# A graph layer on one core: the first two rounds' edge offsets searched in the partition that needs them

## The chip, the core and the metric

The kernel runs on one core of a Trainium2 chip. The metric is the device time of one execution in microseconds (us). Three runs of the kernel before took 808.64, 809.55 and 809.91 us; their median is 809.55. Five engines work side by side, each on its own list of instructions: TensorE (PE), VectorE (DVE), ScalarE (ACT), GpSimd (POOL) and SyncE (SP, which only issues DMAs). Semaphores order them.

## The reference

There are 6250 nodes and 206250 edges, sorted by their target dst; every node has 128 features.

```python
h = x @ W_node.T + b_node
e = edge_attr @ W_edge.T + b_edge
msg = (h[src] + e) @ W_msg.T + b_msg
s = segment_sum(msg, dst)
deg = segment_sum(ones, dst)
out = layernorm(x + s / maximum(deg, 1)[:, None])
```

## The kernel before, in words

Both sums are made with matmuls against one-hot matrices. The nodes are treated in 25 groups of 250 (NB), called rounds; they begin with group 7 (G0), so round m is group (7 + m) mod 25, and N0 = 1750 is the first node of round 0.

**Edge features.** The edges are cut into 101 blocks of 2048 (SUP), from block 27 (FIRST) on. For block t, SP loads 1 MB of edge_attr into one of three buffers (`load_edges`, L375); DVE makes a one-hot of each edge's node relative to the first one of its quarter (`make_onehot`, L725); PE sums (`sum_windows`, L536); ACT copies the result (`copy_windows`, L1167ff); DVE makes `place`; PE puts the window at its nodes (`place_windows`, L549); DVE adds it to `sums_e` (`add_sums`, L736). The relative node numbers come from dst, which ACT loads as `dst_nat`, 2048 edges to a partition; DVE subtracts the first of each quarter and PE turns them.

**Node features.** For each round m, 125 partitions hold the edges of two nodes each. Their 125 entries of src are fetched by an indirect DMA at `clipped_int` (`load_window`, L472). `make_keys` (L764) turns them into a block and a row of x, PE turns these (`turn_keys`), ACT spreads them, DVE makes one-hots for 25 partitions at a time (`make_hots`, L746), a segment, five of which make a round; PE counts them (`count_fill`, L606), ACT moves the counts (`move_bank`), and PE multiplies the counts by x, which is split in three bf16 parts (`apply_counts`, L617). The split of x: ACT copies the high half (`copy_hi`, seven pieces), POOL subtracts it (`split_rest`, L484) and subtracts again (`split_low`, L490), seven times each. The first apply_counts waits for all of them.

**Where a node's edges begin.** This is what the change is about. There are three searches ("jobs"), for the 625 nodes of which rounds 0 and 1 need 500 (job 0), for the later nodes up to 6249 (job 1), and for nodes 0 to 1749 (job 2, called A). In each job 125 partitions have JOB_K nodes each (5, 31, 14). `block_counts` (DVE, L825) and `count_blocks` (PE, L516) count, per partition, the blocks of 128 edges that begin below its first node; `begin_job` (L830) makes an index of it, `load_job` (POOL, L465) fetches 375, 1375 or 750 entries of dst from there, `count_nodes` (DVE) and `sign_counts` (ACT) count in them for each node how many are below it, and `end_job` adds the parts. As a job's partitions hold other nodes than a round's partitions, the result is written to DRAM (`send_starts`, L1188), read back row by row (`fetch_starts`, L1194) and turned by PE (`turn_slots`, L566); `make_slots` (L871) then has slot and index for each round.

**The order.** It is written out by hand: a list of slots u, each engine runs through it in the same order. Slots 0 to 7 (LEAD) treat one edge block each; from slot 8 on, g = u - 8 is a segment, with a block in most of them. So round m has segments 5m to 5m + 4, and apply_counts of round 0 begins with segment 5. On SP, x is loaded behind block 3 (`load_x`, L388), the small weights behind block 6. In slot 6, before, DVE makes the keys of round 0, and behind slot 7 the one-hots of segment 0. POOL's list is: gathers of jobs 0, 1, 2, windows 0 and 1, seven split_rest, seven split_low, the later windows.

## Time and profile before

| what | us |
|---|---|
| median of three runs (808.64 to 809.91) | 809.55 |
| the profiled execution | 809.33 |
| its span, first to last instruction | 807.5 |
| PE busy | 732.5 |
| DVE busy | 634.8 |
| ACT busy | 462.2 |
| POOL busy | 80.5 |

The span is what the profile covers; the 1.8 us between 809.33 and 807.5 lie around it. Times in rows count from the span's start. PE is the engine that works most; where it isn't busy, something else sets the pace, and the slices show where that is.

### The profile page before, as it was taken

The page shows a single profiled execution, that of the slowest core. Times are in us where ns is not written, and L with a number is a line of the kernel's source. Part 1 is how long each engine was busy: PE and PEld are TensorE (multiplying, and loading weights), DVE is VectorE, ACT ScalarE, POOL GpSimd, SP SyncE. Part 2 cuts the span into 40 slices and gives each one's busy share as a digit, 9 for nine tenths or more (in the row PEclk, how much of TensorE's full clock was granted, in tenths as well). Part 3 has the DMA queues.
Part 4 walks back from the last instruction along what each step waited for, and adds up shares of the span by engine and source line. Part 5 has one row for each costly group of instructions (what it writes and reads, how often), then busy time and mean ns, then how long its engine had stood idle before and what let it go on. Part 6 is the DMA issues. An engine that isn't in the chain of part 4 may idle for free.

```text
span 807.5 us, 24927 instructions
## 1 busy us (share of the span) xinstructions
PE 732.5 (91%) x10573; PEld 647.3 (80%) x10573; DVE 634.8 (79%) x1137; ACT 462.2 (57%) x948; POOL 80.5 (10%) x63
## 2 busy tenths in 40 slices
PE   2634569999999999999999999999999999999995
PEld 2423457888988898888988888898898889888895
DVE  7518997699878878887898788878887887888732
ACT  4104955575666566655666576566565656665641
POOL 2113722001000000000000000000000000000000
PEclk9995759899999999999999999999999999999998
DMA  6984426263446424644354454445534653364200
GB/s 206 215 278 156 141 68 179 84 196 122 137 146 223 144 97 162 207 143 162 115 190 151 163 175 125 158 147 197 171 105 134 218 158 130 113 220 134 98 14 16
DMA packets 71806, 121.11 MB, mean 150 GB/s; under 512 B 4717, under 2 KB 17738, under 8 KB 71591
## 3 DMA queue, kind: packets, MB, share of 16 engines
q1 hardware_dynamic: 68462, 115.72, 44.4%
q0 software_dynamic: 2496, 2.84, 1.5%
q8 instruction: 87, 1.43, 0.7%
q10 hardware_dynamic: 734, 0.90, 0.5%
q14 instruction: 27, 0.22, 0.1%
HBM read 116.19 MB, written 3.23 MB: 148 GB/s over the span
## 4 chain that ended last, share of the span: by engine, by line
PE 84%; DVE 8%; DMA 3%; issue 2%; SPq 2%; DVEq 0%; ACT 0%; ACTq 0%
PE x_ps L628 48%; PE count_ps L613 18%; PE win_ps L545 12%; PE win_ps L552 3%; DMA edges<-in_edge_attr_dram 2%; SPq L392 2%; DVE key_hot L754 1%; PE misc_ps L639 1%; PE misc_ps L640 1%; DVE row_hot L754 1%; DVE onehot L728 1%; DVE dve_junk L849 1%; DMA region<-in_dst_dram 1%; DVE region L827 1%; DVE place L734 1%
## 5 line engine op out<-in xcount | busy, mean ns | idle before, releaser
L628 PE MATMUL x_ps<-region,x_rest 128*128 128x250 bf16 x2450 | 450.3, 270 | 0.0
L1227 ACT CAST region<-count_ps 128x490 bf16<-128x490 f32 x625 | 350.8, 574 | 164.4 <-PE count_ps L613 158.8
L628 PE MATMUL x_ps<-region,x_hi 128*128 128x250 bf16 x1225 | 333.0, 272 | 0.0
L754 DVE TENSOR_TENSOR row_hot<-iota_bf,row 125x3200 bf16<-125x3200 bf16 x125 | 229.6, 1837 | 86.5 <-PE count_ps L613 59.7
L613 PE MATMUL count_ps<-key_hot,row_hot 125*128 125x98 bf16 x3125 | 244.7, 210 | 13.4 <-DVE key_hot L754 13.3
L628 PEld LDWEIGHTS x_ps<-region,x_rest 128*128 128x128 bf16 x2450 | 230.0, 98 | 17.7
L613 PEld LDWEIGHTS count_ps<-key_hot,row_hot 125*128 125x128 bf16 x3125 | 200.1, 99 | 43.0 <-issue 18.5
L754 DVE TENSOR_TENSOR key_hot<-iota_bf,key 125x2500 bf16<-125x2500 bf16 x125 | 183.2, 1466 | 0.0
L545 PE MATMUL win_ps<-edges,onehot 128*32 128x128 f32 x3232 | 119.2, 293 | 18.4 <-DMA edges<-in_edge_attr_dram 16.6
L628 PEld LDWEIGHTS x_ps<-region,x_hi 128*128 128x128 bf16 x1225 | 119.1, 97 | 8.0
L545 PEld LDWEIGHTS win_ps<-edges,onehot 128*32 128x32 f32 x3232 | 89.2, 116 | 40.6 <-issue 38.9
L477 POOL DMA_INDIRECT win_src<-in_src_dram,clipped_int x25 | 44.6, 1782 | 539.5 <-DVE key_bf L783 417.7
L1171 ACT COPY win_sb<-win_ps 128x128 f32<-128x128 f32 x101 | 26.9, 266 | 109.2 <-PE win_ps L545 106.4
L728 DVE TENSOR_TENSOR onehot<-iota_bf,rel_col 128x512 f32<-128x512 bf16 x101 | 72.1, 714 | 0.0
L552 PE MATMUL win_ps<-place,win_sb 128*128 128x128 f32 x202 | 43.7, 301 | 15.9 <-ACT win_sb L1171 11.0
L552 PEld LDWEIGHTS win_ps<-place,win_sb 128*128 128x128 f32 x202 | 32.8, 204 | 19.5 <-ACT win_sb L1171 12.6
L744 DVE TENSOR_TENSOR sums_e<-sums_e,win_ps 128x128 f32 x101 | 28.8, 285 | 13.9 <-PE win_ps L552 6.7
L734 DVE TENSOR_SCALAR place<-iota_f,pos 128x128 f32<-128x128 f32 x101 | 33.3, 329 | 0.0
L1239 ACT ACTIVATE stddev<-mean_var,eps_col 125x2 f32<-125x2 f32 x25 | 7.4, 296 | 35.9 <-DVE mean_var L815 35.9
L1245 ACT ACTIVATE y<-y,shift,rstd 125x128 f32<-125x128 f32 x50 | 22.0, 490 | 0.9 <-DVE shift L822 0.9
L793 DVE SCALAR_TENSOR_TENSOR y<-misc_ps,recip,resid 125x128 f32<-125x128 f32 x50 | 15.1, 344 | 8.9 <-PE misc_ps L640 8.9
L639 PE MATMUL misc_ps<-w_both,sums_e 128*125 128x128 f32 x100 | 19.2, 274 | 0.5 <-issue 0.5
(166 smaller groups left out, 345.0 us busy)
## 6 DMA issues: line engine op xcount, KB each, us to landing
edges<-in_edge_attr_dram SPq DMA_DIRECT2D x101, 1024.0 KB, 5.7
resid<-in_x_dram SPq DMA_DIRECT2D x25, 125.0 KB
out_dram<-y SPq DMA_DIRECT2D x25, 125.0 KB
region<-in_dst_dram ACTq DMA_DIRECT2D x1, 768.0 KB
win_src<-in_src_dram,clipped_int POOLq DMA_INDIRECT x25, 6.7
region<-in_L_gnn_W_node_dram SPq DMA_DIRECT2D x1, 64.0 KB
region<-in_L_gnn_W_edge_dram SPq DMA_DIRECT2D x1, 64.0 KB
region<-in_L_gnn_W_msg_dram SPq DMA_DIRECT2D x1, 64.0 KB
```

The costliest lines, as they stand in the source:

```text
L477: pool.indirect_dma_start(out=win_src[:, m % 3, :], out_offset=None, in_=src.rearrange("(r e) -> r e", e=WE), in_offset=bass.IndirectOffse ...
L545: mm = pe.matmul(bank[q * W:(q + 1) * W, 0:D], hot[:, q * J + j, :], edges[:, t % EDGE_SLOTS, q * J + j, :], start=(j == 0), stop=(j == J ...
L552: pe.matmul(l2_ps[t % 2], win_sb[:, t % 2, :], place[:, t % 2, :], start=True, stop=True).then_inc(l2_done, 1)
L613: mm = pe.matmul(count_ps[fill % COUNT_BANKS][:, k * KEYS:(k + 1) * KEYS], row_hot[0:WE, g % 2, f * FILL + k, :], key_hot[0:WE, g % 2, f * ...
L628: mm = pe.matmul(x_ps[m % 2][:, 0:NB], rows, counts[m % 2][:, b, :], start=(n == 0), stop=(n == PARTS - 1))
L639: pe.matmul(to, sums_e[:, first + h * PB:first + (h + 1) * PB], w_both[:, 1, :], start=True, stop=False)
L728: dve.tensor_tensor(onehot[:, t % ONEHOT_SLOTS, :, :], iota_bf[:, 0:W].rearrange("p (a w) -> p a w", a=1).to_broadcast([P, TILES, W]), rel ...
L734: dve.tensor_scalar(place[:, t % 2, :], iota_f[:, :], pos[:, sup_of[t]:sup_of[t] + 1], None, ALU.is_equal).then_inc(place_ready, 1)
L744: dve.tensor_tensor(to, to, l2_ps[t % 2], ALU.add).then_inc(added, 1)
L754: ins = dve.tensor_tensor(hot[0:WE, g % 2, :, :].rearrange("p w (a b) -> p w a b", b=4), iota_bf[0:WE, 0:width].rearrange("p (c a b) -> p ...
L1171: act.copy(win_sb[:, t % 2, :], win_ps[t % 2][:, 0:D]).then_inc(win_copied, 1)
L1227: act.copy(counts[m % 2][:, :, f * FILL * 2:(f + 1) * FILL * 2], count_ps[fill % COUNT_BANKS][:, 0:FILL * KEYS].rearrange("p (n b) -> p b ...
```

## The change

A near search for rounds 0 and 1 takes the place of job 0. Partition p of round r searches itself for the starts of nodes N0 + 250 r + 2p, + 1 and + 2, the three that its slots need, in 275 entries of dst (`begin_near`, `load_near`, `find_near`), three compares on DVE; `take_slots` makes slot and index from them in the same partition. DRAM, ACT and PE's turning have no part in it. The starts are still written to DRAM, in segment 3 (`send_near`), for the degrees of all nodes. Two searches follow, with 32 and 14 nodes a partition and gathers of 1650 and 750 entries. The first local offsets go to PE quarter by quarter, with begin_near(0) between the second and the third. SP waits for all of dst before it loads block 0, and for the first near gather before it loads block 2. x is loaded in two pieces, 21 of its 49 blocks of 128 rows behind edge block 2, the others behind edge block 3. ACT's copies of x go from slots 5 to 7 and segments 0 and 1 to slot 7 and segments 0 to 2. The keys of round 0 move from slot 6 to 5, the one-hots of segment 0 from slot 7 to 6. Each near search has checks that join those already there.

```diff
-JOBS = 3
+JOBS = 2
+NEAR = 2
+NEAR_L = 275
...
-    JOB_K = (5, 31, 14)
-    JOB_N = (N0, N0 + PB * JOB_K[0], 0)
-    JOB_L = (375, 1375, 750)
-    JOB_DVE = (3, 13, 4)
-    JOB_ROWS = (2, B_ROUNDS - 2, G0)
-    JOB_ROUND = (0, 2, B_ROUNDS)
-    LOWEST = ((30, -60), (33, -220), (30, -60))
-    HIGHEST = ((36, 188), (33, 358), (36, 188))
-    TAIL = E - JOB_K[1] * 33 - 175
+
+    NEAR_HIGH = (36, 188)
+    JOB_K = (32, 14)
+    JOB_N = (N0 + NEAR * NB, 0)
+    JOB_L = (1650, 750)
+    JOB_DVE = (13, 4)
+    JOB_ROWS = (B_ROUNDS - NEAR, G0)
+    JOB_ROUND = (NEAR, B_ROUNDS)
...
-            def load_x():
-                sp.wait_ge(x_zeroed, 1)
-                whole = N // P
-                sp.dma_start(x_rest[:, 0:whole, :], x[0:whole * P, :].rearrange("(b p) d -> p b d", p=P)).then_inc(x_in_dram, 16)
-                sp.dma_start(x_rest[0:N - whole * P, whole, :], x[whole * P:N, :]).then_inc(x_in_dram, 16)
+            def load_x(i):
+                whole, half = N // P, 21
+                if i == 0:
+                    sp.dma_start(x_rest[:, 0:half, :], x[0:half * P, :].rearrange("(b p) d -> p b d", p=P)).then_inc(x_in[0], 16)
+                else:
+                    sp.wait_ge(x_zeroed, 1)
+                    sp.dma_start(x_rest[:, half:whole, :], x[half * P:whole * P, :].rearrange("(b p) d -> p b d", p=P)).then_inc(x_in[1], 16)
+                    sp.dma_start(x_rest[0:N - whole * P, whole, :], x[whole * P:N, :]).then_inc(x_in[1], 16)
...
+            sp.wait_ge(dst_in, 48)
             for t in range(NS):
+                if t == 2:
+                    sp.wait_ge(near_in[0], 16)
                 load_edges(t)
-                if t == 3:
-                    load_x()
+                if t in (2, 3):
+                    load_x(t - 2)
...
+            def load_near(r):
+                pool.wait_ge(near_ready[r], 1)
+                pass_waits()
+                pool.indirect_dma_start(out=win_near[r][0:PB, :], out_offset=None, in_=dst.rearrange("(r e) -> r e", e=NEAR_L),
+                                        in_offset=bass.IndirectOffsetOnAxis(ap=near_idx[r][0:PB, 0:1], axis=1)).then_inc(near_in[r], 16)
...
-                pool.wait_ge(src_index_ready, 1 + sum(1 for r in JOB_ROUND[1:] if m >= r))
+                pool.wait_ge(src_index_ready, m + 1 if m < NEAR else NEAR + sum(1 for r in JOB_ROUND if m >= r))
...
+                load_near(r)
+                load_window(r)
             for k in range(JOBS):
                 load_job(k)
-            for m in range(2):
-                load_window(m)
...
-            pe.wait_ge(rel_ready, 1)
             for q in range(Q):
+                pe.wait_ge(rel_ready, q + 1)
...
+            pe.wait_ge(count_taken, 1)
+            count_blocks(1)
...
-                        pe.wait_ge(count_taken, t + 1)
-                        count_blocks(t + 1)
-                    if t == 4:
-                        turn_slots(0)
+                        pe.wait_ge(count_taken, t + 2)
+                        count_blocks(t + 2)
                     place_windows(t)
-                    if t == 6:
+                    if t == 5:
...
+            def begin_near(r):
+                dve.wait_ge(counted, r + 1)
+                link(dve.tensor_scalar(near_base[r][:, 0:1], x_ps[0][0:PB, r:r + 1], float(BLOCK), -float(BLOCK), ALU.mult, ALU.add))
+                dve.sem_inc(count_taken, 1)
+                link(dve.tensor_scalar(near_base[r][:, 1:2], near_base[r][:, 0:1], 0.0, float(E - NEAR_L), ALU.max, ALU.min))
+                dve.tensor_copy(near_idx[r][:, :], near_base[r][:, 1:2]).then_inc(near_ready[r], 1)
...
+            def find_near(r):
+                dve.wait_ge(near_in[r], 16)
+                for i in range(3):
+                    hi = NEAR_HIGH[0] * i + NEAR_HIGH[1]
+                    nodes[0] += 1
+                    if nodes[0] > 2:
+                        dve.wait_ge(node_counted, nodes[0] - 2)
+                    dve.tensor_scalar(dve_junk[nodes[0] % 2][0:PB, 0:hi], win_near[r][0:PB, 0:hi], near_node[r][:, i:i + 1], None, ALU.is_lt, ALU.add,
+                                      accum_out=near_cnt[r][:, i:i + 1]).then_inc(node_counted, 1)
+                dve.wait_ge(node_counted, nodes[0])
+                link(dve.tensor_scalar(near_start[r][:, :], near_cnt[r][:, :], near_base[r][:, 1:2], None, ALU.add))
+                take_slots(r, 1, near_start[r][:, :].rearrange("p (i g) -> p i g", g=1))
...
+            def take_slots(r, rows, found):
+                at = slice(r, r + rows)
+                link(dve.tensor_copy(first_slot[:, :, at], found))
...
-            ins.then_inc(rel_ready, 1)
-            begin_job(0)
-            block_counts(1)
+                ins.then_inc(rel_ready, 1)
+                if q == 1:
+                    begin_near(0)
...
+            block_counts(1)
             dve.wait_ge(pos_turned, 1)
             dve.tensor_copy(base_int[:, :], misc_ps[0:1, 128:128 + NS])
             dve.tensor_copy(check_junk[0:1, 0:NS], misc_ps[0:1, 256:256 + NS])
             link(dve.tensor_copy(pos[:, :], misc_ps[:, 0:NS]))
+            make_place(0)
+            dve.wait_ge(rel_copied, 2)
+            make_onehot(0)
+            make_onehot(1)
+            find_near(0)
             link(dve.scalar_tensor_tensor(check_junk[0:1, 0:NS - 2], misc_ps[0:1, 385:384 + NS - 1], 0.0, check_junk[0:1, 0:NS - 2], ALU.add, ALU.is_lt,
                                           accum_out=viol[0:1, 3:4]))
-            dve.wait_ge(rel_copied, 2)
-            make_onehot(0)
-            make_place(0)
-            make_onehot(1)
+            begin_near(1)
             block_counts(2)
...
-                        begin_job(t + 1)
                     if t == 1:
-                        count_nodes(0, 0, JOB_DVE[0])
-                        end_job(0)
+                        begin_job(0)
+                        block_counts(3)
                     if t == 2:
+                        find_near(1)
+                        begin_job(1)
+                    if t == 3:
                         check_sorted()
-                    if t == 3:
-                        check_job(0)
                     if t == 4:
-                        make_slots(0)
-                    if t == 6:
+                        check_near(0)
+                        check_near(1)
+                    if t == 5:
                         make_keys(0)
...
-                if u == LEAD - 1:
+                if u == LEAD - 2:
                     make_hots(0)
...
+            def send_near():
+                act.wait_ge(src_index_ready, NEAR)
+                for r in range(NEAR):
+                    act.dma_start(starts_dram[N0 + r * NB:N0 + (r + 1) * NB].rearrange("(p k) -> p k", k=2), near_start[r][:, 0:2]).then_inc(near_sent, 16)
...
+                act.wait_ge(x_in[0], 16)
+                if i >= 3:
+                    act.wait_ge(x_in[1], 32)
...
-                        sign_counts(0, JOB_DVE[0], JOB_K[0])
-                    if t == 2:
-                        send_starts(0)
-                    if t == 3:
-                        fetch_starts(0)
-                    if t >= 5:
-                        copy_hi(t - 5)
-                    if t == 6:
+                    if t == 5:
                         spread_keys(0)
+                    if t == 7:
+                        copy_hi(0)
                     continue
...
-                if g < 2:
-                    for i in range(3 + 2 * g, 5 + 2 * g):
+                if g < 3:
+                    for i in range(1 + 2 * g, 3 + 2 * g):
                         copy_hi(i)
-                if g < 3:
-                    sign_counts(1, [13, 19, 25][g], [19, 25, 31][g])
+                    sign_counts(0, [13, 19, 25][g], [19, 25, 32][g])
                 if g == 3:
+                    send_starts(0)
+                    send_near()
```

How it moves instructions. The first place is DVE from where it takes the turned positions to the second block_counts; `misc_ps` is what PE turned, `lent` holds small constants, `region` the gathered entries. Before:

```order
L983 COPY pos<-misc_ps 128x101
L984 SCALAR_TENSOR_TENSOR check_junk,viol<-misc_ps,check_junk 1x99
L728 TENSOR_TENSOR onehot<-iota_bf,rel_col 128x512
L734 TENSOR_SCALAR place<-iota_f,pos 128x128
L728 TENSOR_TENSOR onehot<-iota_bf,rel_col 128x512
L827 TENSOR_TENSOR region<-block_first,lent 101x2000
L832 TENSOR_SCALAR job_base<-x_ps 125x1
```

and now:

```order
L1038 COPY pos<-misc_ps 128x101
L760 TENSOR_SCALAR place<-iota_f,pos 128x128
L754 TENSOR_TENSOR onehot<-iota_bf,rel_col 128x512 x2
L901 TENSOR_SCALAR dve_junk,near_cnt<-region,near_node 125x188
L901 TENSOR_SCALAR dve_junk,near_cnt<-region,near_node 125x224
L901 TENSOR_SCALAR dve_junk,near_cnt<-region,near_node 125x260
L904 TENSOR_SCALAR near_start<-near_cnt,near_base 125x3
L926 COPY first_slot<-near_start 125x3
L927 TENSOR_SCALAR clipped_int<-first_slot 125x1
```

The search of round 0 and its slots stand before the sums of the first window; before, its three compares came in slot 1 and its slots in slot 4.

The second place is DVE at the end of the lead, from a window's sum to the second pair of one-hots. Before, slot 7:

```order
L744 TENSOR_TENSOR sums_e<-sums_e,win_ps 128x128
L734 TENSOR_SCALAR place<-iota_f,pos 128x128
L728 TENSOR_TENSOR onehot<-iota_bf,rel_col 128x512
L754 TENSOR_TENSOR row_hot<-iota_bf,row 125x3200
L754 TENSOR_TENSOR key_hot<-iota_bf,key 125x2500
L754 TENSOR_TENSOR row_hot<-iota_bf,row 125x3200
```

and now, from slot 6 on:

```order
L754 TENSOR_TENSOR onehot<-iota_bf,rel_col 128x512
L780 TENSOR_TENSOR row_hot<-iota_bf,row 125x3200
L780 TENSOR_TENSOR key_hot<-iota_bf,key 125x2500
L763 TENSOR_LOAD base_int
L763 ISA x2
L770 ISA
L770 TENSOR_TENSOR sums_e<-sums_e,win_ps 128x128
L760 TENSOR_SCALAR place<-iota_f,pos 128x128
```

A window's sum stands between the one-hots of segment 0 and those of segment 1.

The third place is SP's first loads. Before:

```order
L373 DMA region<-in_dst_dram 1x1198
L378 DMA edges<-in_edge_attr_dram 128x4x512 x4
L391 DMA x_rest<-in_x_dram 128x48x128
L392 DMA x_rest<-in_x_dram 106x128
L378 DMA edges<-in_edge_attr_dram 128x4x512 x3
```

and now:

```order
L386 DMA region<-in_dst_dram 1x1231
L391 DMA edges<-in_edge_attr_dram 128x4x512 x3
L404 DMA x_rest<-in_x_dram 128x21x128
L391 DMA edges<-in_edge_attr_dram 128x4x512
L407 DMA x_rest<-in_x_dram 128x27x128
L408 DMA x_rest<-in_x_dram 106x128
```

One edge block stands between the pieces of x, and block 4 is still behind both.

## Rows read from the trace of the kernel before

**Rows 1.** The page: busy time, and two of its lines of 40 slices

```profile
PE 732.5 (91%) x10573; PEld 647.3 (80%) x10573; DVE 634.8 (79%) x1137; ACT 462.2 (57%) x948; POOL 80.5 (10%) x63
...
PE   2634569999999999999999999999999999999995
```

**Rows 2.** Stretch from 200 to 400 us: busy by engine, clock, DMA share, GB/s

```profile
200.00:400.00 200.00, 200.00 (x2988) 178.86 (x2987) 168.00 (x269) 125.47 (x256) 12.91 (x7) 1.00 0.48 155
```

**Rows 3.** Timeline of PE, 52 to 80 us: start, length, line, what, [idle before, releaser]

```profile
52.85 1.94 PE L545 MATMUL win_ps<-edges,onehot 128*32 128x128 f32 x32 [16.65 <-DMA edges<-in_edge_attr_dram]
...
56.16 1.94 PE L545 MATMUL win_ps<-edges,onehot 128*32 128x128 f32 x32
...
65.37 0.36 PE L602 MATMUL misc_ps<-ident_bf,row_bf 125*125 125x125 bf16 x1 [3.06 <-DVE key_bf L783]
...
74.68 2.31 PE L613 MATMUL count_ps<-key_hot,row_hot 125*128 125x98 bf16 x25 [5.79 <-DVE key_hot L754]
```

**Rows 4.** Timeline of SP's queue at 35 us

```profile
35.23 9.14 SPq L378 DMA_DIRECT2D edges<-in_edge_attr_dram  x1
```

**Rows 5.** Stretches of the lead: the last two columns are DMA share and GB/s

```profile
10.00:12.00 2.00, 1.54 (x15) 1.55 (x15) 1.96 (x6) 0.00 (x0) 0.00 (x0) 1.00 1.04 386
20.00:22.00 2.00, 2.00 (x28) 1.62 (x21) 1.74 (x1) 0.27 (x1) 0.00 (x0) 1.00 0.07 6
38.00:40.00 2.00, 0.00 (x0) 0.00 (x0) 0.00 (x0) 0.00 (x0) 0.00 (x0) 1.00 1.09 185
42.00:46.00 4.00, 0.00 (x0) 0.00 (x0) 0.00 (x0) 0.00 (x0) 0.00 (x0) 1.00 0.66 141
```

**Rows 6.** Timeline of DVE, 52 to 75 us: the first one-hots for counting

```profile
71.44 1.81 DVE L754 TENSOR_TENSOR row_hot<-iota_bf,row 125x3200 bf16<-125x3200 bf16 x1
...
74.54 1.81 DVE L754 TENSOR_TENSOR row_hot<-iota_bf,row 125x3200 bf16<-125x3200 bf16 x1
```

**Rows 7.** Timeline of DVE, 7 to 30 us: the first use of dst

```profile
7.74 0.18 DVE L960 CAST block_first<-region 101x16 f32<-101x16 int32 x1 [0.45 <-DMA region<-in_dst_dram]
```

**Rows 8.** Line 469, the first two gathers (ns), and all three's time to landing

```profile
L469 POOL DMA_INDIRECT region<-in_dst_dram,job_idx x2: 1294/1798/2302, 14.4 to 24.3; - x2
...
DMA to landing us min/median/max: 5.5/20.3/23.0
```

**Rows 9.** Timeline of DVE: a window's turn on DVE, and a later one-hot

```profile
57.26 0.29 DVE L744 TENSOR_TENSOR sums_e<-sums_e,win_ps 128x128 f32 x1 [0.83 <-DVE slot_low L882]
...
57.66 0.68 DVE L728 TENSOR_TENSOR onehot<-iota_bf,rel_col 128x512 f32<-128x512 bf16 x1
...
61.63 2.38 DVE L728 TENSOR_TENSOR onehot<-iota_bf,rel_col 128x512 f32<-128x512 bf16 x1
```

**Rows 10.** Line 378, loads issued from 50 to 60 us

```profile
DMA to landing us min/median/max: 7.0/7.2/7.3
```

**Rows 11.** Timeline of POOL: the split of x, first subtractions

```profile
59.71 3.73 POOL L484 TENSOR_TENSOR x_rest<-x_rest,x_hi 128x896 f32<-128x896 f32 x2
...
78.66 3.73 POOL L484 TENSOR_TENSOR x_rest<-x_rest,x_hi 128x896 f32<-128x896 f32 x2 [7.83 <-ACT x_hi L1210]
87.84 3.74 POOL L484 TENSOR_TENSOR x_rest<-x_rest,x_hi 128x896 f32<-128x896 f32 x2 [5.45 <-ACT x_hi L1210]
```

**Rows 12.** Timeline of DVE, 101 to 108 us: end of job 1, segment 4's one-hots

```profile
102.81 0.23 DVE L856 TENSOR_TENSOR job_rel<-job_cnt,job_off 125x13 f32<-125x13 f32 x1
...
107.33 1.82 DVE L754 TENSOR_TENSOR row_hot<-iota_bf,row 125x3200 bf16<-125x3200 bf16 x1 [0.24 <-DVE bias_row L928]
```

**Rows 13.** Timeline of ACT: a copy of x, and the last sign pass of segment 2

```profile
67.94 0.94 ACT L1210 COPY x_hi<-x_rest 128x896 bf16<-128x896 bf16 x1
...
99.80 0.77 ACT L1185 ACTIVATE act_junk<-region,job_half 125x578 bf16<-125x578 int32 x1
```

**Rows 14.** Timeline, 104 us on: the first product of counts and x

```profile
115.07 0.41 PE L628 MATMUL x_ps<-region,x_hi 128*128 128x250 bf16 x1
```

**Rows 15.** Line 490: the seven low subtractions (ns, min/median/max)

```profile
L490 POOL TENSOR_TENSOR x_rest<-x_rest x7: 1677/1679/3261, 91.5 to 104.6; 128x896 bf16<-128x896 f32 x7
```

133 lines of the change are left out of this document (73 added, 60 removed).

## Prediction

> **What bounds the kernel now.** I read the page first, then stretches of the trace. The busy line gives TensorE (PE) 732.5 of 807.5 us, and the 40 slices show where it is missing: slices 0 to 5, that is the first 120 us, hold the idle time, from slice 8 on each has a 9 [rows 1]. In the stretch from 200 to 400 us PE is busy 200.00 of 200.00 us [rows 2]. The change touches no matmul of that part, so only what happens before the first rounds run at full pace can change the time: the question is by how much the start of the steady part moves.
>
> The start has three pieces. (a) DMA: behind x on SP's queue stand the edges of block 4, issued at 35.23, and PE stands 16.65 us for them, until 52.85 [rows 3, 4]. I call this moment T. While x moves, the DMA engines are full (share 1.09) at only 185 GB/s, against 386 GB/s while edges move [rows 5]. (b) From T a chain: the offsets of rounds 0 and 1 come back from DRAM and are turned only behind window 4, then their windows of src are fetched, keys made, and PE turns them at 65.37 after 3.06 us of waiting; DVE makes one-hots from 71.44 and PE's first counting starts at 74.68 [rows 3, 6]. (c) From 74.54 on DVE has one-hots, searches and sums in a row. So two points count: T, and the start of the second one-hot pair on DVE, 74.54 [rows 6], which is T + 21.7.
>
> **The early part, before T.** SP now waits for all of dst before the edges of block 0. DVE was through with its preparation at 7.3 and held by dst 0.45 us more [rows 7]; the small operations of a third job (some 0.5 us, an estimate) go too, so the chain starts about 0.9 us earlier. The first gather was issued at 14.4 and landed 5.5 us later [rows 8]. Its index now comes before half of the local offsets, about 1.0 us earlier in all: issue 13.4, landing 18.9. SP holds block 2 for it: its data start near 20.4, where before block 3's started near 22.2 (share 0.07 in 20 to 22 [rows 5]). So the DMA engines set out 1.8 us earlier, but with one more block before them: 1.05 MB at 386 GB/s is 2.7 us. The gathers that fall after this point are larger: before, 124 x 1375 and 125 x 750 words, 1.06 MB; now 124 x 1650, 125 x 750, 125 x 275 and two windows of 125 x 125, 1.46 MB. The 0.4 MB at some 300 GB/s are 1.3 us. x is cut in two, but all of it stays ahead of block 4, so the cut moves nothing for T. **T moves by -1.8 + 2.7 + 1.3 = +2.2 us, to 55.05.** Bounds: in 42 to 46 the share is only 0.66, engines that ran dry while others were behind [rows 5]. That is 1.4 us of full work; if the block laid between the pieces avoids it, and 0.8 us of the gathers slip in beside the x packets, T stays at 52.85. If the engine that is behind now carries more, T may reach 58.
>
> In the shadow of T: DVE now has two find_near (three compares and seven small operations each) and a fourth block_counts, and PE waits for the latter two. PE was idle for 16.65 us there [rows 3], and all of it fits in, if the second near gather comes. Its counterpart, issued at 24.3 among the x packets, took 23.0 us [rows 8]. So I expect it at about 47; behind it come find_near and begin_job (some 3 us, an estimate), add_sums, place and one-hot (1.1 [rows 9]) and PE's placing, to about 52. This is hidden by about 3 us and not more. The Trainium skill (DMA: Bandwidth & Descriptors, Queues, rings and completion order) says that an engine takes turns between its queue rows packet by packet; by that a 0.14 MB gather would come back in about the 5.5 us of the first one, and T would stay 55. No number of the sum needs it.
>
> **From T on.** A block costs PE and ACT 56.16 - 52.85 = 3.3 us [rows 3]. Keys and slots are long there, so nothing waits: blocks 4, 5 and 6 and the turned keys (0.4) end at T + 10.3. add_sums, place and one-hot take 1.1 us on DVE (57.26 to 58.34 [rows 9]) and are through at T + 11.6. The one-hots of segment 0 now stand in slot 6: 3.1 us [rows 6], to T + 14.7. Block 7 lies beside it; its load goes out when window 4 is summed, T + 1.9, and such loads land in at most 7.3 us [rows 10], T + 9.2; PE wants them at T + 10.3, so they are covered, by 1 us. Then 1.1 us for block 7 on DVE, T + 15.8. The first x split on GpSimd falls there; before, three of them fell into the chain [rows 11]: a one-hot took 2.38 us in place of 0.68 [rows 9]. I count half of one collision, 0.7. The second one-hot pair starts at **T + 16.5 and not T + 21.7: 5.2 us gained**. PE's first counting starts at T + 14.9 and not T + 21.8.
>
> **After that**, DVE's list is the same: 17 compares of both jobs, the same one-hots, so the 32.8 us to the one-hots of segment 4 (107.33 - 74.54 [rows 6, 12]) stay. ACT gets two more copies of x in segment 2, 0.94 us each, and one more sign pass of 0.77: 2.7 us [rows 13]. Its passes ended at 99.80 + 0.77 and DVE used them at 102.81 [rows 12, 13], 2.2 us of cover; ACT also starts its segment 0 by 4.7 us earlier where DVE starts 3.0 earlier, so 2.2 + 1.7 - 2.7 = 1.2 us of cover remain. Without it the addition would cost up to 2.7 us. The DMAs of near starts (two issues on ACT) and the waits of later windows lie before round 2 and are needed by nobody earlier; I set them at nothing. **Sum: -5.2 + 2.2 = -3.0 us.** The profiled execution took 809.33 us at a span of 807.5; 806.3 and 804.5 come out. The three runs before have the median 809.55, 0.2 above the profiled one, so I say **806.5 us**.
>
> **Rivals.** *The load tail vanishes.* T stays at 52.85 and the whole 5.2 us come through; with the collision gone too, 5.9 us: 803.7 us. For it speaks the share of 0.66 with work waiting [rows 5], against it that block 4 still stands behind every x packet. *Nothing gained.* The transfers are a floor: block 2 held for near_in, larger gathers among blocks 4 to 7, the second near gather at 52 or later and not at 47. It needs T to move by 5.2, to 58.05; then 809.6. For it: the gathers that were issued beside x took 20.3 and 23.0 us [rows 8]; against it: the added bytes are only 4 us of work. *Slower: x is split too late.* GpSimd splits x in 14 operations, and PE's first product with x at 115.07 needs all [rows 14]. Before, the rests 5 and 6 were done at 91.58. Now their copies stand one segment later; a segment is 87.84 - 78.66 = 9.2 us [rows 11]; with 4.7 us of lead they end at 96.1. Seven low subtractions follow, 1.68 to 3.26 us each [rows 15]; they now lie beside the one-hots of segments 4 and 5. Ready is 107.9 to 118.9, wanted is 115.07 - 3.0 = 112.1. It decides from 2.3 us each; their median was 1.68. At 3.26 PE waits 6.8 us and the kernel is 3.8 us slower: 813.3. For it: a one-hot that met a subtraction grew by 1.7 us and some of GpSimd's nearly doubled [rows 9, 15], and one-hots are the longest that DVE has; against it: half of the low subtractions would have to pay in full. The Trainium skill (SBUF — State Buffer, SBUF: two separate sides) calls the port pair that DVE and GpSimd share an exclusive lock: with two inputs in SBUF beside a reading GpSimd operation, the second one waits for the whole instruction. The step from 0.68 to 2.38 us agrees; by that rule alone all seven would pay and 813.3 would be the time.
>
> **How the numbers follow.** A measurement can tell about 0.2% (1.6 us) from no change. My case (gains of 1.6 to 4.5 us) gets 0.50, the vanishing tail 0.12, nothing gained 0.20, slower 0.18. Faster 0.62, same 0.20, slower 0.18. The range goes from 802.0 (the vanishing tail at 803.7, and the 1.4 us of dry engines gained on top) to 812.0 (two thirds of the late split's wait); about a tenth is left out on each side.
>
> **What would show it.** Right: the sum of window 4 begins at 53 to 57; no wait before the turned keys; first counting 14 to 16 us after T; from there on the same picture as before, moved. PE keeps 200.00 of 200.00 in the middle. Wrong in the early part: window 4 begins after 58, or PE waits for place there (the second near gather). Wrong in the late part: the first product with x waits for GpSimd, or ACT's sign passes are what DVE waits for in segment 2. If T comes before 51 I have misread what the x load costs.

## The result and the profile after

The changed kernel takes 813.62 us (median of 5 runs, 812.78 to 815.12) against 809.55 (808.51 to 810.24, 5 runs) for the kernel before, measured beside it. The ratio is 1.0055, 95% interval 1.004 to 1.007: slower, where 806.5 and a range of 802 to 812 had been predicted. The profiled span grew by 4.3 us, from 807.5 to 811.8.

The page of the changed kernel, busy time and PE's slices (answers to [rows 1]): up to the last slice, which has a 5 before and after, all the idle time is again ahead of slice 8.

```profile
PE 735.5 (91%) x10586; PEld 649.8 (80%) x10586; DVE 640.4 (79%) x1149; ACT 462.1 (57%) x946; POOL 84.8 (10%) x65
...
PE   4525549899999999999999999999999999999995
```

The timeline of PE in the lead, same columns as [rows 3]:

```profile
42.40 1.94 PE L577 MATMUL win_ps<-edges,onehot 128*32 128x128 f32 x32 [3.15 <-DMA edges<-in_edge_attr_dram]
47.34 1.94 PE L577 MATMUL win_ps<-edges,onehot 128*32 128x128 f32 x32 [1.83 <-DMA edges<-in_edge_attr_dram]
...
63.64 1.93 PE L577 MATMUL win_ps<-edges,onehot 128*32 128x128 f32 x32 [12.98 <-DMA edges<-in_edge_attr_dram]
67.92 1.94 PE L577 MATMUL win_ps<-edges,onehot 128*32 128x128 f32 x32 [1.18 <-DMA edges<-in_edge_attr_dram]
71.14 2.31 PE L641 MATMUL count_ps<-key_hot,row_hot 125*128 125x98 bf16 x25
```

These are the sums of windows 4 to 7 (the window of a block of edges has the block's number) and the first counting. Window 4 is summed at 42.40, 10.5 us sooner than before (52.85) and 12.7 sooner than I said. But the long wait for edges did not go: it stands in front of window 6 now, 12.98 us, and the counting starts only 3.5 us earlier than before (74.68).

Stretches of the lead, the last two columns being DMA share and GB/s, as in [rows 5]:

```profile
40.00:44.00 4.00, 1.60 (x32) 1.51 (x32) 2.63 (x13) 0.00 (x0) 1.92 (x2) 1.00 1.00 334
44.00:48.00 4.00, 1.79 (x26) 1.20 (x21) 2.29 (x9) 0.27 (x1) 0.00 (x0) 1.00 1.12 195
48.00:52.00 4.00, 2.28 (x28) 1.64 (x20) 1.13 (x4) 1.32 (x3) 0.00 (x0) 1.00 1.13 171
52.00:56.00 4.00, 0.00 (x0) 0.00 (x0) 0.00 (x0) 0.00 (x0) 0.00 (x0) 1.00 1.06 164
56.00:60.00 4.00, 0.00 (x0) 0.00 (x0) 0.00 (x0) 0.00 (x0) 0.00 (x0) 1.00 0.85 181
```

and the DMA issues from 38 us on (last number: us from issue to landing):

```profile
region<-in_dst_dram,job_idx POOLq DMA_INDIRECT x1, 25.9
...
win_a<-in_dst_dram,job_idx POOLq DMA_INDIRECT x1, 24.6
```

From 24 to 44 us, in which most of x and blocks 3 to 5 move, each stretch of 4 us has 282 to 334 GB/s. The stretch at 160 to 200 GB/s with full engines is still there; it begins at 44, behind x, when the two big gathers, issued at 38.6 and 40.4, are at work. That does not look like x.

The timeline of DVE for the one-hots (L754 makes a block's, L780 those for counting, L760 is place), with [rows 6, 12] as the counterpart:

```profile
73.60 1.81 DVE L780 TENSOR_TENSOR row_hot<-iota_bf,row 125x3200 bf16<-125x3200 bf16 x1
75.33 3.13 DVE L780 TENSOR_TENSOR key_hot<-iota_bf,key 125x2500 bf16<-125x2500 bf16 x1
...
93.50 3.50 DVE L780 TENSOR_TENSOR row_hot<-iota_bf,row 125x3200 bf16<-125x3200 bf16 x1
96.92 3.13 DVE L780 TENSOR_TENSOR key_hot<-iota_bf,key 125x2500 bf16<-125x2500 bf16 x1
100.17 1.50 DVE L760 TENSOR_SCALAR place<-iota_f,pos 128x128 f32<-128x128 f32 x1
101.60 2.18 DVE L754 TENSOR_TENSOR onehot<-iota_bf,rel_col 128x512 f32<-128x512 bf16 x1
...
111.27 2.27 DVE L780 TENSOR_TENSOR row_hot<-iota_bf,row 125x3200 bf16<-125x3200 bf16 x1 [0.24 <-DVE bias_row L982]
```

and of POOL, the split of x:

```profile
71.10 1.89 POOL L513 TENSOR_TENSOR x_rest<-x_rest,x_hi 128x896 f32<-128x896 f32 x1 [28.88 <-ACT x_hi L1275]
75.12 5.09 POOL L513 TENSOR_TENSOR x_rest<-x_rest,x_hi 128x896 f32<-128x896 f32 x2 [2.13 <-ACT x_hi L1275]
84.30 3.92 POOL L513 TENSOR_TENSOR x_rest<-x_rest,x_hi 128x896 f32<-128x896 f32 x2 [4.08 <-ACT x_hi L1275]
93.44 5.30 POOL L513 TENSOR_TENSOR x_rest<-x_rest,x_hi 128x896 f32<-128x896 f32 x2 [5.22 <-ACT x_hi L1275]
98.70 13.17 POOL L519 TENSOR_TENSOR x_rest<-x_rest 128x896 bf16<-128x896 f32 x7
```

The second pair starts at 73.60, 0.9 us earlier than before (74.54). From there to segment 4's one-hots it is 111.27 - 73.60 = 37.7 us; it was 32.8. Wherever POOL is at x, a place takes 1.5 to 1.7 us and not 0.28, a block's one-hot 2.2 to 2.4 and not 0.68, a key_hot 3.13 and not 1.45. **The sum: -0.9 + 4.9 = +4.0 of the 4.3 us.** PE's first product with x comes at 119.47 (115.07 [rows 14]), 4.4 us later; it waits for DVE's one-hots, not for x. From there to the end of the span the two kernels take the same time, 692.3 and 692.4 us. In the stretch from 200 to 400 us PE is busy 199.75 of 200 us.

The time behind that first product is not quite the same in all the profiled runs that follow: it lies between 688.6 and 693.1 us, with no order that the edits explain. So where two versions differ by 2 to 4 us, the traces' times up to the first product with x say how much of it is the edit's.

### The profile page after: what moved, and what is told of

Read it like the earlier page. It is cut to its first block, busy times and chain, and to the rows that moved or that the text cites. A ratio compares the mean times of both kernels' runs of the same rounds, so it can differ in the third digit from the quotient of the medians.

```text
span 811.8 us, 24971 instructions
## 1 busy us (share of the span) xinstructions
PE 735.5 (91%) x10586; PEld 649.8 (80%) x10586; DVE 640.4 (79%) x1149; ACT 462.1 (57%) x946; POOL 84.8 (10%) x65
## 4 chain that ended last, share of the span: by engine, by line
PE 84%; DVE 9%; DMA 4%; issue 2%; DVEq 0%; ACT 0%; ACTq 0%
PE x_ps L656 48%; PE count_ps L641 17%; PE win_ps L577 12%; DMA edges<-in_edge_attr_dram 3%; PE win_ps L584 3%; DVE key_hot L780 2%; PE misc_ps L667 1%; PE misc_ps L668 1%; DVE onehot L754 1%; DVE row_hot L780 1%; DVE region L853 1%; DVE dve_junk L882 1%; DVE place L760 1%; PE x_ps L549 1%; DMA region<-in_dst_dram 1%
## 5 line engine op out<-in xcount | busy, mean ns | idle before, releaser
L780 DVE TENSOR_TENSOR row_hot<-iota_bf,row 125x3200 bf16<-125x3200 bf16 x125 | 230.0, 1840 | 86.5 <-PE count_ps L641 59.7
L656 PEld LDWEIGHTS x_ps<-region,x_rest 128*128 128x128 bf16 x2450 | 230.1, 98 | 17.7
L780 DVE TENSOR_TENSOR key_hot<-iota_bf,key 125x2500 bf16<-125x2500 bf16 x125 | 185.2, 1481 | 0.0
L754 DVE TENSOR_TENSOR onehot<-iota_bf,rel_col 128x512 f32<-128x512 bf16 x101 | 72.2, 715 | 0.0
L760 DVE TENSOR_SCALAR place<-iota_f,pos 128x128 f32<-128x128 f32 x101 | 32.5, 322 | 0.0
L549 PE MATMUL x_ps<-ones_bf,region 101*125 101x1 bf16 x64 | 7.4, 245 | 17.5 <-DVE region L853 17.5
L549 PEld LDWEIGHTS x_ps<-ones_bf,region 101*125 101x125 bf16 x64 | 7.1, 227 | 18.7 <-DVE region L853 9.8
```

What stands on the lines that cost most here:

```text
L549: mm = pe.matmul(x_ps[0][0:PB, k:k + 1], before_hot[k][0:NS, j, :], ones_bf[0:NS, 0:1], start=(j == 0), stop=(j == TILES - 1))
L656: mm = pe.matmul(x_ps[m % 2][:, 0:NB], rows, counts[m % 2][:, b, :], start=(n == 0), stop=(n == PARTS - 1))
L754: dve.tensor_tensor(onehot[:, t % ONEHOT_SLOTS, :, :], iota_bf[:, 0:W].rearrange("p (a w) -> p a w", a=1).to_broadcast([P, TILES, W]), rel ...
L760: dve.tensor_scalar(place[:, t % 2, :], iota_f[:, :], pos[:, sup_of[t]:sup_of[t] + 1], None, ALU.is_equal).then_inc(place_ready, 1)
L780: ins = dve.tensor_tensor(hot[0:WE, g % 2, :, :].rearrange("p w (a b) -> p w a b", b=4), iota_bf[0:WE, 0:width].rearrange("p (c a b) -> p ...
```

## Experiments on the split of x

Theory P: all of the loss behind the second pair is POOL's split, now beside DVE's densest stretch, because ACT's copies of x, which release it, were moved from slots 5 to 7 and segments 0 and 1 to slot 7 and segments 0 to 2.

**The copies put back** (in the changed kernel), `e1_copies_back`:

```diff
-                    if t == 7:
-                        copy_hi(0)
+                    if t >= 5:
+                        copy_hi(t - 5)
...
-                if g < 3:
-                    for i in range(1 + 2 * g, 3 + 2 * g):
+                if g < 2:
+                    for i in range(3 + 2 * g, 5 + 2 * g):
```

> The changed kernel, with ACT's seven copies of x where they were before: slots 5, 6, 7 and segments 0 and 1. Theory P (the split of x on GpSimd, moved from the lead into the segments, costs DVE about 5 us there): the stretch from the second one-hot pair on DVE to the one-hots of segment 4, 37.7 us in the changed kernel, goes back to 33 to 34 us and the time to about 809 (808 to 810). Rival (it is ACT's extra work in segment 2, or the near searches, and the place of the split is nothing): 813 to 814.

Measured: 809.73 us, ratio to before 1.0017 (1.0003 to 1.003), against 1.0055: 3 to 4 us less than the changed kernel. The stretch is 31.9 us (75.95 to 107.89). The part of the change that cost time is the place of seven copies. But the time only comes back to the kernel before. The pair starts at 75.95, 2.4 us later than in the changed kernel, because two of POOL's subtractions now fall ahead of it, where a place took 1.69 us and a key_hot 3.13. So with its copies in the old place the change gains nothing either.

**All copies in slots 4 and 5**, `v1_split_in_lead`:

```diff
+                    if t == 4:
+                        for i in range(3):
+                            copy_hi(i)
                     if t == 5:
                         spread_keys(0)
+                        for i in range(3, 7):
+                            copy_hi(i)
...
```

The copies at slot 7 and in segments 0 to 2 go.

> The changed kernel with all seven copies of x in slots 4 and 5, so that GpSimd splits x while PE and DVE stand for the edges of block 6. Theory P: GpSimd is through by about 70 us, the stretch from the second one-hot pair to the one-hots of segment 4 shrinks to 24 to 28 us, the time is 800 to 805. Rival (the segments are paced by ACT's sign passes and the split's place matters little): 809 to 813.

Measured: 803.22 us, ratio 0.9932 (0.9904 to 0.996), faster than both kernels. POOL splits from 45.19 to 77.56. Four of the seven first subtractions (54.99 to 62.39) fall where DVE waits 8.45 us for window 6. The low ones, 62.35 to 77.56 and not done by 70 as expected, meet DVE at the first pair (row_hot 3.30 us, key_hot 2.93), so the second pair starts no earlier than in e1, 2.3 us later than in the changed kernel. In the stretch only that pair's row_hot meets POOL, and it is 25.4 us (75.94 to 101.32).

**The converse, in the kernel before**: copies at slot 7 and segments 0 to 2, `e4_before_copies_late`.

> The kernel before, with only the copies of x moved as in the change: slot 7 and segments 0 to 2 in place of slots 5 to 7 and segments 0 and 1. Theory P: slower by 2 to 5 us, 811 to 815 (the lead gains about 2 us that the segments lose again and more). Rival (place is nothing): 809 to 810.

Measured: 810.69 us, ratio 1.0023 (1.0005 to 1.0041). That is 1.9 us by the ratio, a little under the 2 to 5 expected. The second pair starts at 72.57, 2.0 us sooner than in the kernel before. The stretch grows only from 32.8 to 33.8 us, because POOL's operations met few one-hots in it: one row_hot took 3.29 us and one 2.08, while every place and key_hot up to 92 us took its undisturbed time. The loss stands behind the stretch, where the low subtractions (98.72 to 113.02) reach segment 4's one-hots: row_hot 2.27 us, key_hot 2.93, place 1.50. The first product with x comes at 117.25, and it was 115.07. So the same edit costs about 2 us there and 3 to 4 here. By the rows this hangs on which of DVE's operations POOL then meets.

## Experiments on the slow stretch

**A quarter of the big gathers**, `e2_gather_quarter`: 32 of the 125 partitions are fetched, the others hold a constant. The offsets of rounds 2 and later follow from the constant, and the fallback, the slow path for offsets that are not as assumed, is kept off.

```diff
-                n = PB - 1 if k == 0 else PB
+                n = 32
```

> The changed kernel; the two big gathers fetch 32 partitions instead of 124 and 125, the others hold a constant, and the flag for the slow path is always 0, so the offsets of later rounds are wrong. Theory G (the gathers, 1.2 MB in 249 long rows, make the slow stretch of DMA from 44 to 62 us, and x is not slow): that stretch shrinks to about a quarter, window 6 starts at 50 to 54 and not at 63.6, the time falls by 6 to 10 us to 804 to 808. Rival X (x's short rows or the tiny bias loads make it slow): the stretch stays at 160 to 180 GB/s and window 6 starts at 60 to 63; the time falls by 1 to 3 us.

Measured: 800.52 us, ratio 0.9896 (0.9874 to 0.9918). Window 6 comes at 53.19 with no wait. The stretch from 44 to 60 us:

```profile
44.00:60.00 16.00, 11.07 (x138) 8.22 (x138) 8.46 (x28) 2.95 (x7) 0.80 (x2) 1.00 1.06 333
```

The mechanism held; the gain on the changed kernel (0.9896 against 1.0055, 12.9 us) is larger than the 6 to 10 us expected. Window 6 comes 10.5 us earlier, as expected, the second pair as much (62.98), and segment 4's one-hots 12.1 us earlier (99.21).

**The same bytes by plain transfers, the same rows by indirect ones.** `e5_direct` takes fixed rows, one behind the other, without an index; `e8_indirect_apart` takes the same rows with an index that holds their places; `e9_indirect_overlap` lets the rows overlap (row p starts at word 1056 p and 448 p). All three fetch other words of dst than the search wants; the fallback is off. The edit of e5:

```diff
-                pool.indirect_dma_start(out=win_of[k][0:n, :], out_offset=None, in_=dst.rearrange("(r e) -> r e", e=JOB_L[k]),
-                                        in_offset=bass.IndirectOffsetOnAxis(ap=job_idx[k][0:n, 0:1], axis=1)).then_inc(job_win_in[k], 16)
+                pool.dma_start(win_of[k][0:n, :],
+                               dst[0:n * JOB_L[k]].rearrange("(r e) -> r e", e=JOB_L[k])).then_inc(job_win_in[k], 16)
```

> The changed kernel, but its two big gathers fetch the same number of bytes by plain transfers on GpSimd's queue: each partition gets a row of 1650 (750) words at a fixed place of dst, the rows do not overlap, and no index is read; the waits and the place in the program are the same. The words are not the ones wanted, so the offsets from round 2 on are not right, and the fallback is kept off. Theory I (what is slow is the indirect form, or windows of dst that overlap): 44 to 60 us runs at over 260 GB/s, window 6 is summed at 52 to 55 and not at 63.6, and the time is 801 to 806. Theory B (1.2 MB on a second queue in long rows into 124 partitions are slow in any form): 44 to 60 stays at 160 to 200 GB/s, window 6 at 61 to 65, time 812 to 815.

> The changed kernel, its two big gathers still indirect, but with fixed indices: row p starts at word 1650 p (750 p), so the rows lie one behind the other, as in the plain transfers of the run before. The offsets from round 2 on are not right and the fallback is kept off. The plain form took the slow stretch away; two things had changed with it, the indirect form and the overlap of the rows. Theory F (the indirect form is slow): 44 to 60 us stays at 160 to 210 GB/s, the gathers land 20 us or more after their issue, window 6 at 60 to 65, time 808 to 814. Theory O (overlapping windows are slow): over 260 GB/s, window 6 at 50 to 55, time 799 to 804.

> As the run before, but row p starts at word 1056 p (448 p): the rows overlap as the wanted ones do (by 594 of 1650 and 302 of 750 words), and all start at multiples of 256 or 64 bytes. Theory F: as the run before, 160 to 210 GB/s in 44 to 60, time 808 to 814. Theory O: slow here and fast in the run before. If both are fast, what is slow is the start of a row at any word and not at an even boundary.

| version | time, us | ratio to before (95%) | window 6 at | the gathers land after |
|---|---|---|---|---|
| e5_direct | 801.94 | 0.9907 (0.9872 to 0.9942) | 54.74 | 10.9, 12.4 us |
| e8_indirect_apart | 811.46 | 1.0028 (1.001 to 1.0046) | 63.83 | 25.7, 24.3 us |
| e9_indirect_overlap | 811.05 | 1.0031 (1.0014 to 1.0049) | 56.59 | 26.1, 24.9 us |

It is the indirect form: e5 and e8 fetch the same rows. In e9 window 6 came at 56.59, but window 7 then waited 7.96 us more and came at 67.66, as in e8 (67.54) and in the changed kernel (67.92): the lateness goes to one block or the next. The plain form is not free either: in e5 window 5 came at 51.49, after a wait of 5.66 us, and in the changed kernel at 47.34. The DMA queues from 38 to 66 us (packets, MB, share of 16 engines), first of e5_direct (plain):

```profile
DMA packets 4667, 8.74 MB, mean 312 GB/s; under 512 B 538, under 2 KB 928, under 8 KB 4664
...
q1 hardware_dynamic: 4376, 7.44, 79.3%
q0 software_dynamic: 288, 1.26, 18.2%
```

and of e8_indirect_apart:

```profile
DMA packets 3962, 6.32 MB, mean 226 GB/s; under 512 B 1008, under 2 KB 1393, under 8 KB 3961
...
q1 hardware_dynamic: 3161, 5.04, 72.6%
q0 software_dynamic: 800, 1.26, 23.1%
```

q1 is the queue that SP's loads use, q0 the gathers'. 1.26 MB of the same rows are 288 packets in the plain form and 800 in the indirect one, and the packets under 512 bytes go from 538 to 1008. The edges on q1 suffer too: 28 us of 16 engines, times 0.726, over 3161 packets is 103 ns for each, against 81 ns in the plain run, at about the same 1.6 to 1.7 KB. These slower packets are the larger part of the loss: at 81 ns each, q1's time in e8 would have held some 4000 packets, so some 850 of the 1215 by which q1 falls short are theirs, while q0's own share grew only from 18.2% to 23.1%. Why a packet of q1 is slower beside the indirect ones no row shows.

**Was it the same in the kernel before?** `e10_before_plain` is that kernel with the edit of e5 for jobs 1 and 2 (other words of dst, fallback off).

> The kernel before, its gathers of jobs 1 and 2 fetched by plain transfers of the same bytes (fixed rows, no index); their offsets are not right and the fallback is kept off. My prediction read 28 to 48 us of the kernel before as x being slow (185 GB/s). If it was the indirect gathers there too, x and the edges behind it move at over 260 GB/s, window 4 is summed at 42 to 47 and not at 52.85, and the time is 798 to 804. If x was slow by itself, window 4 stays at 50 or later and the time at 806 or more.

Measured: 802.65 us, ratio 0.9939 (0.9923 to 0.9956). The wait for block 4 on PE, where [rows 3] had 52.85 after 16.65:

```profile
46.77 1.94 PE L548 MATMUL win_ps<-edges,onehot 128*32 128x128 f32 x32 [10.77 <-DMA edges<-in_edge_attr_dram]
```

and the stretch in which x moves, first of the kernel before, then of e10:

```profile
28.00:44.00 16.00, 4.82 (x64) 3.29 (x56) 7.25 (x22) 0.53 (x2) 1.22 (x1) 1.00 1.02 193
```

```profile
28.00:44.00 16.00, 4.97 (x68) 3.43 (x60) 7.04 (x24) 0.53 (x2) 0.57 (x1) 1.00 1.05 265
```

So 6.1 us of T in the kernel before were the gathers. The drop from 265 to 193 GB/s, which I had read as the price of x, was two gathers that happened to move with it. The rest of the wait, 10.77 us, stays: x and block 4 behind it still have to move.

**Two smaller parts.** `e6_small_later` issues the weights and biases behind block 7 (`if t == 7: load_small()`), `e7_x_whole` both pieces of x behind block 3 (`if t == 3: load_x(0); load_x(1)`).

> The changed kernel, but the weights and biases (three transfers of 64 KB in rows of 512 bytes, and some of 4 bytes a row) are issued behind the edges of block 7 and not of block 6. Theory S (a good part of the slow stretch from 44 to 60 us is these small packets): the rate there rises over 240 GB/s, window 7 is summed by 62, the time is 806 to 810. Theory G (the big gathers make it): window 6 stays at 62 to 65, the time at 812 to 815.

> The changed kernel, but both pieces of x are issued behind the edges of block 3, one after the other, as x was before. Theory G (the gathers of dst set the start, the cut of x moves nothing): window 3 is summed some 2 us earlier, windows 4 to 7 where they were within 1.5 us (42.4, 47.3, 63.6, 67.9), the time 812 to 815. Rival (a block between the pieces costs or saves): windows 6 and 7 move by 2 us or more, and the time with them.

Measured for e6: 810.64 us, ratio 1.0023 (1.0003 to 1.0044), between the times of both theories, with the slow stretch still at 159 to 196 GB/s and window 6 at 61.34 (63.64). The small loads don't make the stretch. They cost little: of the some 3 us only 1.3 stand ahead of the first product with x (118.19), the rest behind it, where the edit changed nothing. For e7: 812.25 us, ratio 1.0048 (1.0032 to 1.0065), a time that can't be told from the changed kernel's. Window 3 came no earlier (36.05) and window 6 at 65.32, 1.7 us later, a little more than the 1.5 allowed.

## Versions made from this

**Gathers behind block 6** (v1, and POOL waits for block 6's landing before it issues them), `v2_gathers_behind`, and the same kernel once more, `v2_again`:

```diff
+            pool.wait_ge(edge_in[0], 16 * 3)
             for k in range(JOBS):
                 load_job(k)
```

> The version with all of x's copies in slots 4 and 5, and the two big gathers are issued only when the edges of block 6 have landed. Theory G: block 6 lands some 6 us after its issue, window 6 is summed at 50 to 54 and not at 59.3; the gathers then meet block 7 alone. If the loss does not just move on, the second one-hot pair starts by 68, nothing waits for the gathers, and the time is 796 to 801. Rival (it only moves on: block 7 or the first searches wait as long): window 7 is summed at 66 or later, or DVE waits for the gather in segment 0, and the time stays at 802 to 805.

> The version with the gathers behind block 6, once more. If the stall of DVE belongs to this order of GpSimd's work, one place operation stands again for 20 us or more, until the last of GpSimd's 14 split operations; if it was a chance of that execution, none stands over 4 us and the time is under 803.

Measured: 805.59 us, ratio 0.9961 (0.994 to 0.9982), slower than v1 and outside both expectations, and 807.65 in the one run of v2_again. Window 6 came at 48.54, even before the 50 to 54 expected, and window 7 at 54.00; then something that I had not foreseen. DVE and POOL of v2_gathers_behind:

```profile
54.41 21.81 DVE L761 TENSOR_SCALAR place<-iota_f,pos 128x128 f32<-128x128 f32 x1
76.14 0.68 DVE L755 TENSOR_TENSOR onehot<-iota_bf,rel_col 128x512 f32<-128x512 bf16 x1
```

```profile
50.52 1.22 POOL L492 DMA_INDIRECT win_a<-in_dst_dram,job_idx  x1 [0.30 <-issue]
51.76 12.91 POOL L513 TENSOR_TENSOR x_rest<-x_rest,x_hi 128x896 f32<-128x896 f32 x7
64.64 11.50 POOL L519 TENSOR_TENSOR x_rest<-x_rest 128x896 bf16<-128x896 f32 x7
```

A place operation of 0.28 us stood for 21.8 us, until the last of POOL's 14 operations ended at 76.14. v2_again shows the same, 21.58 us: it belongs to this order of work.

**A gate against it**, `v6_gate`: POOL waits, behind its gathers, for the one-hot that DVE makes behind window 7's sum (`pool.wait_ge(onehot_ready, 10)`).

> The version with the gathers behind block 6 (805.6), in which a place operation stood 21.8 us until GpSimd's 14th split operation was through; now GpSimd waits behind its gathers until place and one-hot of window 7 are done. If the stall came from the split starting right behind the issue of the gathers, no operation of DVE takes over 4 us, the second pair starts at 62 to 68, time 794 to 799. If DVE can be kept out by any unbroken run of GpSimd's operations, another one of its operations stands for 10 us or more and the time is 802 to 808.

Measured: 803.86 us, ratio 0.9942 (0.9924 to 0.9959). No operation of DVE stood over 3.1 us, and the second pair started at 59.50. But the gathers still took 23 us, and DVE then waited for the first one:

```profile
72.72 0.58 DVE L884 TENSOR_SCALAR_CACHE_REDUCE dve_junk<-region,job_node 125x358 bf16<-125x358 int32 x1 [10.03 <-DMA region<-in_dst_dram,job_idx]
```

and after it the low subtractions met its one-hots. The stall was gone, the gain was given back: the expectation failed by its time (794 to 799) and held by its operations. It doesn't fully clear the cause either: from 59.67, when POOL's split began, to 83.39 DVE had no place to do.

**The split as early as x allows**, `v3_split_early` and `v3_again`: ACT copies in slots 1 and 3, and POOL's list is

```diff
+            load_near(0)
+            load_window(0)
+            load_near(1)
+            split_rest(0)
+            split_rest(1)
+            load_window(1)
+            load_job(0)
+            load_job(1)
+            pool.wait_ge(onehot_ready, 7)
+            split_rest(2)
+            pool.wait_ge(keys_ready, 1)
+            for i in range(3, 7):
+                split_rest(i)
+            for i in range(7):
+                if i == 5:
+                    pool.wait_ge(onehot_ready, 9)
+                split_low(i)
```

> All of x's copies in slots 1 and 3 on ScalarE; GpSimd splits x piece by piece as early as it is there (two pieces ahead of the second src window, one behind window 4, the rest behind the keys of round 0), the big gathers where the changed kernel has them. Window 6 still waits for its edges until 58 to 62 (it is the gathers that hold it), but DVE's one-hots from there on are at 1.8 and 1.45 us and not at 3.3 and 2.9: the second pair starts at 67 to 72 (75.9 with the copies in slots 4 and 5), segment 4's one-hots at 92 to 97, time 796 to 800. Rival (DVE was not what followed behind: block 7 lands late, PE waits for it): second pair at 75, time 802 to 804.

> The best version once more, with more rounds: 793 to 798, ratio to before 0.981 to 0.988; window 7 at 66 to 69, second one-hot pair at 71 to 73.

Measured: 795.5 us, ratio 0.9846 (0.9807 to 0.9886), and in a second set of runs 798.44, ratio 0.9881 (0.9854 to 0.9908), window 7 at 69.15 and the second pair at 73.39, each a little beyond what was expected of it. The first product with x comes at 103.74 and 105.05, 15.7 and 14.4 us before the changed kernel's; by the ratios the two sets gain 16.9 and 14.1. POOL in v3_split_early:

```profile
29.15 4.68 POOL L513 TENSOR_TENSOR x_rest<-x_rest,x_hi 128x896 f32<-128x896 f32 x2 [4.68 <-ACT x_hi L1283]
...
48.95 7.84 POOL L513 TENSOR_TENSOR x_rest<-x_rest,x_hi 128x896 f32<-128x896 f32 x4 [1.01 <-DVE key_bf L817]
56.74 14.75 POOL L519 TENSOR_TENSOR x_rest<-x_rest 128x896 bf16<-128x896 f32 x7
```

The split is through at 71.5, the second pair starts at 72.10, segment 4's one-hots at 96.00: 23.9 us for what took 37.7. The first pair still met POOL, against the expectation (row_hot 3.29 us, key_hot 2.93), but it stands in the wait for window 7, where it costs nothing. Window 7 still comes at 66.89, after 10.46 us of waiting for edges, which is the gathers' part and stays. This version beats both kernels.

**Three tries on top.** `v4_early_and_behind` has the gathers behind block 6 too, with the last five low subtractions held until DVE has made the one-hot behind window 7's sum; `v5_second_last` issues the second gather behind the split; `v7_small_later` loads the weights behind block 7.

> As the run before, and the big gathers are issued behind block 6's landing (49 us), with the rest of the splits behind the keys and the last five subtractions behind the one-hot of window 9, so that DVE gets its turn between them. Window 6 at 48 to 50, window 7 at 54 to 56, no operation of DVE over 5 us, second pair at 62 to 68; then DVE waits for the first big gather until about 70. Time 793 to 800. If a place operation again stands until GpSimd's last subtraction (21.8 us in the version with the gathers behind), the time is 804 to 808 and the waits that were put in don't help.

> The version that splits x early (795.5), with the second gather (job 1) issued behind the whole split, at some 70 us; it is wanted at 103. One gather is left beside blocks 6 and 7: its packets end some 6 us earlier, window 7 is summed at 58 to 63 and not at 66.9, the second one-hot pair starts at 66 to 70 (72.1), time 790 to 794. Rival (DVE beside GpSimd's split sets the pair, not the edges): second pair at 71 to 72, time 795 to 796.

> The best version with the weights and biases issued behind block 7. In the changed kernel this edit freed window 6 by 2.3 us (61.3 for 63.6) and window 7 by 1.0. If block 7 is held by packets of the small loads ahead of it, window 7 is summed 1 to 3 us earlier than in the run before, time 793 to 795 where it has 795.5; if the gathers alone hold it, no difference over 0.2% to the run before.

Measured: 797.58 (ratio 0.9855, 0.9824 to 0.9887), 797.77 (0.9872, 0.9849 to 0.9896) and 799.36 us (0.9879, 0.9851 to 0.9906). None is told apart from v3. In v7 window 7 came 2.8 us earlier than in v3_again (66.35 for 69.15), the second pair did not (73.99 for 73.39), since DVE's key_hot and place there met POOL's last operations. In v4 a place stood again, for 9.35 us from 51.80, until POOL paused at 61.06, and window 7 came at 62.00 and not at 54 to 56. v5 is a miss of its own: with only one gather in the way window 7 came at 68.78, no earlier, and that gather took 27.1 us, while the second, issued at 72.04, landed in 7.2; from 72 to 80 us one block of edges was issued and all queues together moved 271 GB/s. The same gather (750 words a partition) had taken 24.6 us in the changed kernel. So the time of a gather follows what moves beside it more than its bytes, and one is enough to spoil the lead.

## Why the prediction was wrong

- **The early part up to the first gather: right.** Issue at 13.40 (13.4 predicted), landing after 4.3 us at 17.7 (18.9), block 2 issued at 17.8.
- **"While x moves ... only 185 GB/s": this step failed, and with it T.** The rate was put down to x; e10 has 265 GB/s where the kernel before had 193, with x moving all the same, and e5 and e8 show that it is the indirect form of the gathers of dst that slows the others. They are issued at 38.6 in the changed kernel and not at 24.3, so x and blocks 4 and 5 got ahead of them. T is 42.40, and not 55.05; it lies below my whole range for it, and "if T comes before 51 I have misread what the x load costs" was the right alarm.
- **The second near gather at about 47: wrong**, it landed 10.1 us after its issue, at 32.4. The 23 us came from a big gather, and this one was small. The 10.1 are also not the 5.5 that I had worked out by the Trainium skill (DMA: Bandwidth & Descriptors, Queues, rings and completion order).
- **Blocks 4, 5 and 6 at 3.3 us each and block 7 covered by 1 us: wrong**, for the same reason. Block 6 landed 25.5 us after its issue, where [rows 10] gave 7.3. The slow stretch had not been removed, it had moved behind T.
- **The second pair at T + 16.5 = 71.55: 2.0 us off** (73.60), from two errors that nearly cancel, by luck: T 12.7 us too late, what follows it 14.7 too short. The step gave 0.9 of the 3.0 us.
- **That the 32.8 us stay: this term cost the sign.** It was 37.7. I had counted half of one collision between POOL and DVE ahead of the pair and none after it, although [rows 9] showed the size, 1.7 us for one, and the diff showed the copies moved by one to two segments. I followed the copies only to the question whether x is ready in time. The 32.8 us held such meetings too (a row_hot of 3.29 us in the kernel before); v1 and v3, whose split is nearly or wholly through by then, have 25.4 and 23.9. With e1 the stretch is 31.9 and the time that of the kernel before: there the meetings ahead of the pair take back what had been gained. So the slow stretch behind T left a gain of only 0.9 us, and the copies turned it into a loss.
- **The rival "x is split too late" had the right edit, the right time (813.3) by luck, and the wrong mechanism.** The low subtractions were done at 111.87, PE wanted x at 119.47 and did not wait for it. The loss fell on DVE, whose one-hots PE waits for: 9.06 us before the counting at 114.97. The Trainium skill (SBUF — State Buffer, SBUF: two separate sides) says that the loser of the shared port pair blocks for the whole instruction. The rows agree for one collision (0.28 to 1.7, 1.45 to 3.13 us, beside POOL's operations of some 1.9). v2 shows more than that: a wait over some twelve instructions in a row.
- **Hidden and steady parts: right.** ACT's extra passes did not hold DVE (the last compare ends at 106.71, job_rel starts at 106.75), the near search cost nothing, and PE keeps its pace in the middle.

Open: why a place stood for 21.8, 21.6 and 9.35 us in v2, v2_again and v4, and never over 2.3 in the others. In all three a run of POOL's subtractions begins right behind the issue of a big gather; the gated version differs in that and shows no stall, which fits but does not settle it.

## What to carry to other kernels

Before a slow stretch of DMA is put down to the largest transfer in it, list all that moves in it and ask which of them are also there when it is fast. A good test is to replace one by a plain transfer of the same bytes. When a change moves work of an engine that shares something with the bound engine, price every meeting at the new place: being ready in time is only half of the question. And an idle stretch of the engine that shares with it is where such work belongs: here the ratio to before went from 1.0055 to 0.985 or 0.988, some 14 to 17 us.

## What the runs showed of the hardware

- An indirect gather of 124 to 125 rows of 3 to 6.6 KB took 2.8 times the packets of the plain transfer of the same rows (800 for 288 in two gathers). Beside two of them the DMA engines moved 188 GB/s (changed kernel, 44 to 66 us), beside two plain ones 306 (e5_direct), at a share of 0.98 and 0.96. The indirect ones landed after 20 to 27 us beside x or several blocks of edges, one of them after 7.2 us at 72 us in v5, with one block beside it.
- A DVE operation of 0.28 us stood beside back-to-back POOL operations for up to 21.8 us (v2_gathers_behind), and for 1.5 to 1.7 us where it met one of them (changed kernel).
- ACT's copies of x (0.94 us each) and DVE's compares into an accumulator (0.80 us) took the same time with POOL at work and without (changed kernel; e1 and v1).
